# Two banks of Sx then four of k and v, and the context's eighths one at a time, in an attention layer on one Trainium2 core

## The reference

```
q, k, v = w_qkv @ groupnorm(x)
context = softmax(k over pixels) @ v^T ;  content_out = context^T @ q
Sx = einsum('ndxy,xid->nixy', q4, Px)   ;  Yh = einsum('nixy,neiy->nexy', Sx, v4)
Yh = batch norm of Yh over all images, heads and pixels
Sy = einsum('ndxy,yid->nixy', q4, Py)   ;  rel_pos_out = einsum('nixy,nexi->nexy', Sy, Yh)
out = x + w_out @ (content_out + rel_pos_out) + b_out
```

## Time and profile before

| | us |
|---|---|
| median of 3 timed runs | 2899.37 (2896.96 to 2903.32) |
| the profiled execution | 2909.64 |
| its span | 2907.8 |
| TensorE busy in it | 2536.0 |
| VectorE, ScalarE, GpSimd busy | 2006.5, 1689.8, 1405.4 |
| first phase, about | the first 1808 us |

### The profile page before, as it was taken

One profiled execution on the slowest core, in us unless ns is written; L12 is line 12 of the kernel. 1 busy time (PEld: TensorE's weight loads), 2 busy tenths in 40 slices (PEclk: granted clock), 3 DMA queues, 4 the chain that ended last, 5 costly groups with the idle time before them and its releaser, 6 DMA issues. The chain is left out here.

```text
span 2907.8 us, 125746 instructions
## 1 busy us (share of the span) xinstructions
PE 2536.0 (87%) x57972; PEld 2048.1 (70%) x57972; DVE 2006.5 (69%) x3062; ACT 1689.8 (58%) x2984; POOL 1405.4 (48%) x617
## 2 busy tenths in 40 slices
PE   4898898898898899898898896689899898989897
PEld 3687787787687677787787784666676767676674
DVE  7577677677567567667667554787687868687774
ACT  3565655665655565565565663556565646566663
POOL 0424434434424334344334433776767767576761
PEclk9999999999999999999999997799999999999999
DMA  2422533533522532542535424577768777777763
GB/s 99 138 63 76 146 79 76 152 73 90 144 66 75 132 93 68 128 104 70 147 83 126 109 65 114 131 198 194 186 178 232 176 205 172 212 189 208 186 175 110
DMA packets 448639, 382.75 MB, mean 132 GB/s; under 512 B 307312, under 2 KB 374128, under 8 KB 448112
## 3 DMA queue, kind: packets, MB, share of 16 engines
q1 hardware_dynamic: 429680, 341.14, 46.8%
q10 hardware_dynamic: 18432, 33.56, 3.2%
HBM read 205.79 MB, written 168.82 MB: 129 GB/s over the span
## 5 line engine op out<-in xcount | busy, mean ns | idle before, releaser
L843 POOL TENSOR_TENSOR k_f<-k_f,negmax 128x1024 f32<-128x1024 f32 x128 | 304.7, 2408 | 860.1 <-DVE negmax L810 860.1
L457 PE MATMUL bank<-w_hi,x_hi 128*128 128x256 f16 x2048 | 575.4, 281 | 9.3 <-DVE x_lo L734 7.7
L457 PE MATMUL bank<-w_hi,x_lo 128*128 128x256 f16 x2048 | 569.2, 278 | 1.1 <-issue 1.0
L457 PE MATMUL bank<-w_lo,x_hi 128*128 128x256 f16 x2048 | 569.8, 278 | 0.0
L1290 POOL TENSOR_TENSOR x_f<-x_f,ones 128x1024 f32<-128x1024 f32 x127 | 286.0, 2252 | 229.0 <-DMA x_f<-y_scratch 224.5
L1242 DVE TENSOR_TENSOR yb_lo<-x_f,yb_hi 64x1024 f16<-64x1024 f32 x192 | 371.4, 1934 | 31.3 <-ACT yb_hi L1156 28.2
L749 DVE TENSOR_TENSOR v_lo<-bank,v_hi 128x256 f16<-128x256 f32 x512 | 213.7, 421 | 259.6 <-ACT v_hi L601 257.5
L600 ACT ACTIVATE k_f<-bank 128x256 f32<-128x256 f32 x512 | 200.3, 391 | 298.7 <-PE bank L457 295.7
L457 PEld LDWEIGHTS bank<-w_hi,x_hi 128*128 128x128 f16 x2048 | 297.6, 145 | 16.6 <-issue 8.3
L457 PEld LDWEIGHTS bank<-w_lo,x_hi 128*128 128x128 f16 x2048 | 299.9, 146 | 5.1 <-issue 1.5
L457 PEld LDWEIGHTS bank<-w_hi,x_lo 128*128 128x128 f16 x2048 | 297.8, 145 | 5.3 <-issue 1.5
(11 more groups left out here) (152 smaller groups left out, 8207.2 us busy)
## 6 DMA issues: line engine op xcount, KB each, us to landing
y_scratch<-yst SPq DMA_DIRECT2D x256, 256.0 KB, 4.4
x_f<-y_scratch SPq DMA_DIRECT2D x256, 256.0 KB, 6.3
q<-q_scratch SPq DMA_DIRECT2D x256, 256.0 KB, 5.0
x_f<-x SPq DMA_DIRECT2D x64, 512.0 KB, 5.6
q_scratch<-q_hi SPq DMA_DIRECT2D x128, 256.0 KB
q_scratch<-q_lo SPq DMA_DIRECT2D x128, 256.0 KB
x_res<-x SPq DMA_DIRECT2D x128, 256.0 KB, 6.7
out<-x_res ACTq DMA_DIRECT2D x128, 256.0 KB, 4.3
```

What stands on the lines that cost most here:

```text
L457: mm = pe.matmul(outs, lhs[a], rhs[m], start=first and n == 0, stop=last and n == 2, **kw)
L843: pool.tensor_tensor(kk, kk, negmax[:, :].unsqueeze(1).to_broadcast([P, 8, P]), ALU.add).then_inc(shifted, 1)
```

## The change

The order of the items in the 23 mixed turns is now two Sx and four kv, four times over. The eighths of the context are issued one at a time, after j = 0, 1, 3, 4, 5, 7, 8 and 9. `context_out` stands after item 11 in place of 9, and SyncE's `store_context` behind the stores of Yh items 4 and 5. Nothing is added or left out: the program has as many instructions on TensorE as before.

```diff
-                for i in range(0, SX, 2):
-                    order += [("sx", hp, i), ("sx", hp, i + 1), ("kv", hp + 1, i), ("kv", hp + 1, i + 1)]
-                order += [("kv", hp + 1, i) for i in range(SX, KV)]
+                for i in range(0, SX, 2):
+                    order += [("sx", hp, i), ("sx", hp, i + 1)] + [("kv", hp + 1, 2 * i + k) for k in range(4)]
...
+            CONTEXT_AT = {0: 0, 1: 1, 3: 2, 4: 3, 5: 4, 7: 5, 8: 6, 9: 7}
...
                         store_ys(2, 3)
+                        next_x(2)
+                        store_ys(4, 5)
                         if before:
                             store_context(b * HP + (hp - 1))
-                        next_x(2)
-                        store_ys(4, 5)
...
-                            if j < 8 and j % 2 == 1 and not (order is first_turn and h == 0):
-                                context_piece(b, h - 1, j - 1)
-                                context_piece(b, h - 1, j)
+                            if j in CONTEXT_AT and not (order is first_turn and h == 0):
+                                context_piece(b, h - 1, CONTEXT_AT[j])
...
-                            if j == 9 and not (order is first_turn and h == 0):
+                            if j == 11 and not (order is first_turn and h == 0):
                                 context_out(dve, b * HP + (h - 1))
```

## The result

The changed kernel took 2862.0 us (median of 6 runs, 2852.64 to 2883.07) against 2898.84 us for the kernel before beside it (6 runs, 2893.93 to 2903.6): a ratio of 0.988, 95% interval 0.986 to 0.990. Two later comparisons of the same pair gave 0.991 (0.989 to 0.993) and 0.991 (0.988 to 0.994). The change gains some 26 to 37 us. The forecast was a gain of 13 us, and the range ended at 2869 us: the sign was right, the size was not, by a factor of two to three.

The account below looks back on a forecast made before the run. TensorE was taken to bound the first phase, with idle time from instruction-block fetches. The terms, -24, +20, +6, -4, -6, +1, summed to -7 us, or -13 with the second at +14: median 2887 us, range 2869 to 2908.

Parts of the forecast that it names:

- Term 1: First q item to the matmul spreading the maximum: q items between the first eighths cut instruction-fetch stalls, -24 us.
- the longest under 2 us: Sign in the profile after: the context matmuls' longest issue wait under 2 us, their total falling from 39.9 to about 22.
- Term 2: From q4 to the last Yh pair: eighths moved behind q4 and q5 add fetch stalls, +20 us, taken as +14.
- Term 6: Last head pair: VectorE, near its limit until Sx is through, takes back part of the stall changes, +1 us.
- Term 3: Between q3 and q4: the matmul spreading the maximum newly waits for VectorE's diagonal, +6 us.
- Term 4: Mixed Sx and k/v items: stalls behind the first Sx pair go, nine of them, -4 us.
- Term 5: TensorE's clock in the first phase: three or four fewer half-clock falls behind context stalls, -6 us.
- The eighths' stalls go wholly: Rival: a q item between eighths suffices for the fetch nearly everywhere; -33, 2866 us, chance 0.11.
- The stalls move and grow: Rival: slow blocks between q4 and the last Yh pair make added stalls outweigh the savings; +8, 2907 us, chance 0.21.
- Nothing moves: Rival: only average instruction density over the whole q stage counts; -1, 2898 us, chance 0.23.
- Stalls apart from the order: Rival: stalls do not hang on instruction order, leaving only the spreading matmul's new wait; +6, 2905 us, chance 0.03.

Follow-up runs that it names:

- the shifted pair: Kernel before and changed kernel, each with 32 extra small matmuls (128 instructions, half a block) at the start: 2915.6 us (1.003) and 2885.4 us (0.993).
- early eighths: Changed kernel, two eighths put back in pairs among q0 to q3, none behind q4 or q5: 0.995; with q's first store and the spreading matmul later: 0.986.
- the late q store: q's first store in head pairs 0 to 2 put off behind stores of Yh items 4 and 5: kernel before 1.001; changed kernel 0.985, again 0.984.

## Why the prediction was wrong

**Term 1 (-24 us): right.** Issue stalls of place A fell by 31 us by my sums, and by 27 to 30 us in the repeats and with the eighths alone. The mechanism (blocks of 256 instructions, and a q item between eighths as breathing space) stands. The prediction had two distances between stalls for it; in the whole first phase of before 76 of the 80 distances between issue stalls of 0.7 us or more, counted in weight loads and matmuls, lie within 12 of a multiple of 256, and 64 of 70 in after. The page still has 455 packets, the shift of the blocks changed nothing, and the kernel without any eighth among q and Yh has no context stall at all. Only "the longest under 2 us" missed, at 2.3 us.

**Term 2 (taken +14 us), with Term 6 (+1 us): the step that failed.** As a stall, Term 2 had about the right size: place B rose by 19 us in the profiled run (by 8 to 22 us in the repeats and with the eighths alone). (Of its three blocks the middle one, 4.9 us in the text, is 5.0 us between the ends of the stalls at 728.68 and 733.70 us, which changes nothing.) What failed is that this stall was booked as a loss on the path with nothing against it. The step took 96 instructions more in B, "not new work but moved", and never asked what stood at the place they had left and whom that place had kept waiting; Term 6 then held VectorE's waits where they were, but for +1 us. The runs showed these waits falling. Without those in place A, where Term 3's new wait stands, they were 34.4 us before and 21.8 us after, 17.4 and 20.9 us in the repeats and 13.8 us with the eighths alone: 13 to 21 us less, and 28.2 against 40.2 us in the shifted pair. They vary with other edits too: four kernels with the eighths as before have 27 to 40 us. Term 6 put them all in the last head pair; 22 of the 34 us are there, and 11 in the third.

The two pairs with early eighths show the same from the other side, but they are no measurement of the +14 us alone, since the early arrangement also gives up a part of Term 1. By the prediction's own rule a dense run of 336 instructions would bring 13 of Term 1's 24 us, without Term 2 and without the wait of Term 3. That is an estimate of 9 us in favour of early eighths in the first pair, and of 3 us in the second, where neither kernel has that wait. Measured are 13 and 9 us against them, so 22 and 12 us are missing, where VectorE's waits rose by 14 and 20 us.

**Term 3 (+6 us): the wait came, a price did not show.** L563 waited 4.7 us in 13 places for the diagonal, in after's last head pair for up to 1.1 us, where the text had 1.4. With the wait gone the kernel was not faster in one pair (0.993 against 0.991) and 6 us faster in another, with intervals that overlap. In the kernel without eighths ahead of the matmul the same wait was 76 us: the two eighths that stayed on this way (there were four) are what covers it.

**Term 4 (-4 us): the number is right within its error, the reason is not.** With the order of items alone the gain is 9 us (16 to 2), but the issue stalls behind the first Sx pair, nine of which were to go, stayed at 39 us there and in after. That the number came all the same is luck. VectorE's waits were 7.8 us shorter in the one profiled execution; whether they are the reason is not shown, since these waits vary by some us between kernels in which nothing bears on them.

**Term 5 (-6 us): mis-sized.** The busy time for the same matmuls fell by 18.2 us in the profiled run, and by 12 to 13 us in the two repeats (2523.1 and 2524.4 us against 2536.0). Most comes with the eighths (2525.7 us with them alone, 2533.5 us with the order of items alone). I had counted falls behind context stalls only; in the clock's record of the first phase TensorE spent 138 us at the lower level before and 109 us after (120 and 133 us in the repeats). This varies between executions of one kernel by as much as the term is large, so a smaller error cannot be told. In the pair of profiled executions the busy time is 10 us of the miss (16 us less in the first phase where 6 were booked), and no run tells how much of that is the change.

**Term 6 (+1 us): wrong sign,** as said with Term 2.

**The sum.** By the runs, all that the eighths do (terms 1, 2, 3, 6 and most of 5) is -17 us, where the prediction had -9 for it (-24, +14, +6, +1 and the -6), and the items' order is -9 where it had -4. That is -26 us by the ratios, as the two repeats have it. The first comparison's is -35 by its ratio and -37 by its medians, and no run tells why it is larger; its interval from 0.986 to 0.990 overlaps theirs only at their lower ends. So how far the forecast was off is itself known to some 10 us only: 13 us by the repeats, 24 by the first. That the eighths feed VectorE sooner, and that the prediction left this out, is shown by the waits in every trace and by the two pairs. How the miss divides between this and the busy time is known for the two profiled executions only. There the first phase lost 41 us: 31 at A, 6 at C, 7 of VectorE's waits (12 or 13 without the new one) and 16 of busy time, against 19 more at B.

**The rivals.** *The eighths' stalls go wholly* gave 2866 us, nearest to the result, but not by its mechanism: A kept 24 of 54 us. Its number was luck. *The stalls move and grow* was right that they move and wrong that this decides. *Nothing moves* fell with the intervals. *Stalls apart from the order* fell with the kernel that has no eighths among q and Yh. The Trainium skill's rule that I weighed ("Runtime: NRT & Kernel Launch", section "Instruction fetch mechanics": the cost of crossing a block is mostly hidden) stays contradicted for this stretch: issue stalls were 157 us before and still 139 us after over the first phase.

## What to carry to other kernels

An instruction that is moved has two prices, one where it arrives and one where it left: ask of each place which engine is fed next by what follows, not only how dense the place becomes. Work that no other engine waits for may well stand behind the work that feeds the engine that will be late (9 and 13 us in the two pairs here), but not as late as it can: with one eighth behind each q item the gain was gone. And before adding stalls up as a cost, ask what the same stretch would wait for without them: the late q store took 19 us of stalls from B and gave nothing on the kernel before, and gave 19 us of time on the changed one. Why it pays on one and not on the other is not shown.

## What the hardware showed beside this

A q store's packets slow the supply of instructions: with the store moved away, stalls at Yh fell from 33.9 to 14.2 us at the same order of instructions on TensorE. In the trace of before the stretch from 723 to 738 us, with its three slow blocks, has 4096 packets of 256 bytes, as many as one such store of 1 MB makes.

Putting items of 128*128 and of 128*64 by turns cost 0.24 us for each pair (above), where 128*64 beside 128*64 cost nothing; a change to 64*64 costs the same 0.09 us.

VectorE's operations are at times held up while GpSimd works. In the kernel with late eighths, an operation of VectorE that takes 1.22 us elsewhere in the turn took 3.38 us, from 862.13 to 865.51, and GpSimd's pair of operations ended at 864.43, some 1.1 us before it:

```profile
851.12 1.22 DVE L714 TENSOR_TENSOR x_lo<-x_f,x_hi 128x1024 f16<-128x1024 f32 x1
862.13 3.38 DVE L714 TENSOR_TENSOR x_lo<-x_f,x_hi 128x1024 f16<-128x1024 f32 x1
```

```profile
859.30 5.13 POOL L841 TENSOR_TENSOR k_f<-k_f,negmax 128x1024 f32<-128x1024 f32 x2
```

It looks as if VectorE's work began only when GpSimd's had ended. It is no single case: of the 36 such operations of VectorE 11 took 3.37 to 3.39 us in the trace of before and 7 in that of after, and each of these began about 0.5 us after such an operation of GpSimd and ended 1.1 us behind it. Those that began 0.16 us ahead of a GpSimd operation (17 in before) took their 1.22 us. So the order of the eighths also changes how often the two meet: 7 times in all three traces of the changed kernel, 11 times in both traces with early eighths (8 in the one beside the second). It cannot be the whole reason for the early eighths' loss, since it was 7 times too in the run with the context's closing and store alone, which gained nothing. The q_lo for which Sx waited at 866.17 us was next in VectorE's queue, so this is the next thing to look at there.
